# Second gating layer of the second cycle in three fp32r passes, with the first half's first turn moved between first-layer tiles

## What is computed

```python
def _coupling_net(h, w1, b1, w2, b2, w3, b3, w4, b4):      # 512 -> 512 -> 256 -> 128 -> 1
    h = _gelu(h @ w1 + b1)
    h = _gelu(h @ w2 + b2)
    h = _gelu(h @ w3 + b3)
    return jax.nn.sigmoid(h @ w4 + b4)

gf = _global_net(x.mean(axis=1, keepdims=True), ...)
out = x
for _ in range(3):
    tf = _coupling_net(out, ...)
    combined = 0.7 * gf + 0.3 * tf
    coupling = 0.1 + adaptive_range * (combined - 0.5) * 2.0
    out = out + coupling * _twist(out)
```

## Time and profile before

| | before |
|---|---|
| runs, median (lowest to highest) | 1707.92 us (1707.28 to 1707.93) |
| profiled execution: its time, its span | 1706.81 us, 1705.0 us |
| granted TensorE clock, mean | 0.998 |
| TensorE matmuls busy | 1680.3 us (99%) |
| VectorE busy | 1475.7 us (87%) |
| ScalarE busy | 1272.9 us (75%) |
| GpSimd busy | 680.1 us (40%) |

### The profile page before, as it was taken

The page is one execution under the profiler, slowest core; times in us unless marked ns, Lnnn a source line. Parts: engine busy times, 40 slices in busy tenths (PEclk is TensorE's granted clock), DMA queues, the critical chain, the costliest instruction groups (busy, mean ns, idle before and its releaser), DMA issues. The chain is left out here.

```text
span 1705.0 us, 33568 instructions
## 1 busy us (share of the span) xinstructions
PE 1680.3 (99%) x12344; PEld 1283.1 (75%) x12344; DVE 1475.7 (87%) x2615; ACT 1272.9 (75%) x2249; POOL 680.1 (40%) x649
## 2 busy tenths in 40 slices
PE   8999999999999999999999999999999999999997
PEld 7888887777777777777777777777786685775864
DVE  6666666999999999999999999999788978969968
ACT  4233235999999999999999999999765576466556
POOL 3545443332388552586432785465323010100100
PEclk9999999999999999999999999999999999999999
DMA  9989966765477754667764675666515313412301
GB/s 317 355 309 333 340 248 177 170 168 135 140 190 183 142 140 107 149 204 143 162 150 121 150 198 128 142 134 154 182 35 160 91 50 99 139 50 52 113 26 50
DMA packets 165922, 270.09 MB, mean 158 GB/s; under 512 B 26736, under 2 KB 79216, under 8 KB 165760
## 3 DMA queue, kind: packets, MB, share of 16 engines
q1 hardware_dynamic: 110416, 158.84, 29.3%
q0 software_dynamic: 54768, 108.05, 27.0%
q10 hardware_dynamic: 576, 1.05, 0.2%
HBM read 179.48 MB, written 84.21 MB: 155 GB/s over the span
## 5 line engine op out<-in xcount | busy, mean ns | idle before, releaser
L1103 DVE CUSTOM_DVE_ANT_0 a_neg<-a_sc_ps,am 128x1024 f32<-128x1024 f32 x512 | 621.9, 1215 | 2.0 <-PE a_sc_ps L935 1.8
L1043 ACT ACTIVATE a_prob<-a_neg,a_row_min 128x1024 f32<-128x1024 f32 x512 | 585.6, 1144 | 14.7 <-DVE a_row_min L1103 8.6
L949 PEld LDWEIGHTS a_tr_ps<-ident,a_prob 128*128 128x128 f32 x4096 | 461.1, 140 | 89.2 <-issue 53.2
L949 PE MATMUL a_tr_ps<-ident,a_prob 128*128 128x128 f32 x4096 | 519.8, 274 | 0.9 <-ACT a_probT L1021 0.9
L1078 DVE COPY a_probT<-a_tr_ps 128x512 f32<-128x512 f32 x512 | 350.6, 685 | 36.9 <-PE a_tr_ps L949 35.3
L1021 ACT ACTIVATE a_probT<-a_tr_ps 128x512 f32<-128x512 f32 x512 | 303.8, 594 | 35.7 <-PE a_tr_ps L949 16.0
L831 POOL DMA_DIRECT2D a_q_st<-q_parts x144 | 79.5, 557 | 166.5 <-PE a_sc_ps L935 131.6
L935 PE MATMUL a_sc_ps<-k_first,a_q_st 96*128 96x512 f32 x384 | 126.3, 427 | 0.1
L935 PE MATMUL a_sc_ps<-a_k_st,a_q_st 96*128 96x512 f32 x384 | 126.0, 426 | 0.0
L969 PE MATMUL a_o_ps<-a_probT,a_v 128*32 128x256 f32 x2048 | 123.6, 382 | 0.6 <-ACT a_o L1032 0.6
L969 PE MATMUL a_o_ps<-a_probT,v_first 128*32 128x256 f32 x2048 | 123.8, 382 | 0.0
(11 more groups left out here) (246 smaller groups left out, 3299.7 us busy)
## 6 DMA issues: line engine op xcount, KB each, us to landing
a_q_st<-q_parts POOLq DMA_DIRECT2D x144, 128.0 KB, 3.9
k_first<-k_parts POOLq DMA_DIRECT2D x24, 512.0 KB, 8.4
a_k_st<-k_parts POOLq DMA_DIRECT2D x24, 512.0 KB, 7.6
a_m_raw<-mask SPq DMA_DIRECT2D x24, 512.0 KB, 4.9
a_adj_raw<-adj SPq DMA_DIRECT2D x24, 512.0 KB, 6.0
k_parts<-p_out_hi SPq DMA_DIRECT2D x32, 256.0 KB, 4.0
k_parts<-p_out_lo SPq DMA_DIRECT2D x32, 256.0 KB, 5.2
v_all<-p_v_out SPq DMA_DIRECT2D x8, 1024.0 KB, 4.8
```

The costliest lines, as they stand in the source:

```text
L949: last = pe.transpose(tr_ps[:, bank(u, half), j * P:(j + 1) * P], prob[:, r % NPROB, t * P:(t + 1) * P], ident[:])
L1043: act.activation(prob[:, r % NPROB, :], neg[:, r % 2, :], ACT.Exp, scale=-1.0, bias=row_min[:, r % 2:r % 2 + 1], accum_out=row_sum[:, r // ...
L1103: dve.tensor_tensor_reduce(out=neg[:, r % 2, :], in0=sc_ps[:, r % 2, :], in1=am[:, 2 * qb + qt, :], scale=-1.0, scalar=3.4e38, op0=ALU.add ...
```

## The change

The second cycle's second layer is done in three passes too. ScalarE makes two Gelus of each of its tiles (high part to `u_hi_second`, whole value to `u_second`, which lies in the memory of `u_hi`), and VectorE subtracts them in `split_u(b, 1, j)`. The first turn (n = 0, j = 0) moves ahead: its `layer2` stands after the second half's first-layer tile 1 and accumulates in `tr`, its `layer3` stands after tile 2 and writes to `z4`, its `layer4` after tile 3. ScalarE's and VectorE's lists follow. For k = 1 to 4 ScalarE's list now has all tiles of `h1` of the next turn ahead of `h2_half` of turn k. VectorE's list is regular: `second_cycle`, two tiles of `turned`, `split_u`, two tiles of `turned`. Two loads wait for a later turn. Cut to its core:

```diff
-    SPLIT = (0, 2)
+    SPLIT = (0, 1, 2)
-        h1_second = [... f_h1_second{j} ... F32, offset=SB_AM + 8192 * j ...]
+        u_hi_second = [... f_u_hi_second{j} ... F32R, offset=SB_AM + 8192 * j ...]
+        u_second = [... f_u_second{j} ... F32, offset=u_hi_at[j] ...]
+        u_lo_second = [... f_u_lo_second{j} ... F32R, offset=u_hi_at[j] ...]
...
-                            sp.wait_ge(z2_ready, 2 * turn(b, 0, 0) + 2)
+                            sp.wait_ge(z2_ready, 2 * turn(b, 1, 0) + 2)
...
-                    pool.wait_ge(z2_ready, 2 * turn(b - 1, 0, 1) + 2)
+                    pool.wait_ge(z2_ready, 2 * turn(b - 1, 1, 1) + 2)
...
             def layer2(b, n, j, tiles):
+                out = tr if n == 0 and j == 0 else acc[:, 2 * j:2 * j + 2]
                 if n == 0 and 0 in tiles:
                     if j == 0:
-                        pe.wait_ge(own_read, 2 * ET * NJ * (b + 1))
+                        pe.wait_ge(xT_lo_ready, ET * NJ * (b + 1))
                     else:
                         pe.wait_ge(shared_read, 4 * ET * NJ * (b + 1))
...
-                            last = pe.matmul(acc[:, 2 * j + m, :], w2[:, t, ms], h1_second[j][:, t, :], start=t == 0, stop=t == ET - 1)
+                        last = three_pass(pe, out[:, m, :], w_hi[:, t, ms], w_lo[:, t, ms], high[:, t, :], low_part[:, t, :],
+                                          t == 0, t == ET - 1)
...
                 global_layer1(b, 1)
+                layer2(b, 0, 0, (0, 1))
+                global_layer2(b)
+                layer2(b, 0, 0, (2, 3))
+                global_layer3(b)
                 first_layer(b, 1, 2)
+                layer3(b, 0, 0)
                 first_layer(b, 1, 3)
-                layer2(b, 0, 0, (0,))
-                global_layer2(b)
-                for k in range(NJ * CYCLES):
+                layer4(b, 0, 0)
+                layer2(b, 0, 1, (0,))
+                for k in range(1, NJ * CYCLES):
                     n, j = k // NJ, k % NJ
                     layer2(b, n, j, (1, 2, 3))
-                    if k == 0:
-                        global_layer3(b)
                     layer3(b, n, j)
...
-                if n == 1:
-                    act.activation(h1_second[j][:, m, :], u[j][:, m, :], ACT.Gelu, ...).then_inc(h1_ready, 1)
-                    return
-                act.activation(u_hi_third[j][:, m, :], ...)
-                act.activation(u[j][:, m, :], ...).then_inc(h1_ready, 1)
+                act.activation((u_hi_second if n == 1 else u_hi_third)[j][:, m, :], ...)
+                act.activation((u_second if n == 1 else u)[j][:, m, :], ...).then_inc(h1_ready, 1)
...
                 first_cycle_h1(b, 1, 1)
                 act.wait_ge(gz2_ready, b + 1)
                 act.activation(g2[:], z4[:, 1, 2:3], ACT.Gelu, bias=small.gb2[:]).then_inc(g2_ready, 1)
+                act.wait_ge(gz3_ready, b + 1)
+                act.activation(g_tanh[:], z4[:, 1, 3:4], ACT.Tanh, ...).then_inc(g3_ready, 1)
+                h2_half(b, 0, 0, 0)
+                h2_half(b, 0, 0, 1)
+                read_own(b, 1, 2)
+                h3_all(b, 0, 0)
+                first_cycle_h1(b, 1, 2)
+                read_own(b, 1, 3)
                 first_cycle_h1(b, 1, 3)
-                for k in range(NJ * CYCLES):
+                gate(b, 0, 0)
+                for k in range(1, NJ * CYCLES):
                     n, j = k // NJ, k % NJ
-                    if k == 3:
-                        next_h1(0)
+                    if k <= NJ * (CYCLES - 1):
+                        for m in range(ET):
+                            h1(b, (k - 1) // NJ + 1, (k - 1) % NJ, m)
                     h2_half(b, n, j, 0)
                     h2_half(b, n, j, 1)
-                    next_h1(1 if k == 3 else 0)
                     h3_all(b, n, j)
-                    if k < 3:
-                        next_h1(1, 2)
-                        gate(b, n, j)
-                        next_h1(3)
-                        continue
-                    if k == 4:
-                        next_h1(1)
-                    next_h1(2, 3)
...
                 split_w2(b)
+                split_u(b, 0, 0)
                 add_shared(b, 1, 1)
-                add_shared(b, 1, 2)
-                split_u(b, 0, 0)
-                add_shared(b, 1, 3)
-                split_u(b, 0, 1)
+                split_u(b, 0, 1, (0, 1))
                 dve.wait_ge(g3_ready, b + 1)
                 dve.tensor_scalar(base[:], ...).then_inc(base_ready, 1)
+                add_shared(b, 1, 2)
+                split_u(b, 0, 1, (2,))
+                add_shared(b, 1, 3)
+                split_u(b, 0, 1, (3,))
...
                         second_cycle(b, j)
-                        turned(b, 0, ((0, 1, 2), (3,))[j])
-                        if j:
-                            turned(b, 1, (0, 1))
+                        turned(b, j, (0, 1))
+                        split_u(b, 1, j)
+                        turned(b, j, (2, 3))
                     elif n == 1:
                         third_cycle(b, j)
-                        if j == 0:
-                            turned(b, 1, (2,))
-                        split_u(b, 2, j, (1,))
-                        if j == 0:
-                            turned(b, 1, (3,))
-                        split_u(b, 2, j, (2, 3))
+                        split_u(b, 2, j, (1, 2, 3))
```

More of the change, by code:

```diff
@@ L1159, in ffn_phase @@
         pair_lo = sb("f_pair_lo", [P, 2, CH], F32R)
-        h1_second = [nc.alloc_sbuf_tensor_at(f"f_h1_second{j}", [P, ET, CH], F32, offset=SB_AM + 8192 * j) for j in range(NJ)]
+        u_hi_second = [nc.alloc_sbuf_tensor_at(f"f_u_hi_second{j}", [P, ET, CH], F32R, offset=SB_AM + 8192 * j) for j in range(NJ)]
+        u_second = [nc.alloc_sbuf_tensor_at(f"f_u_second{j}", [P, ET, CH], F32, offset=u_hi_at[j]) for j in range(NJ)]
+        u_lo_second = [nc.alloc_sbuf_tensor_at(f"f_u_lo_second{j}", [P, ET, CH], F32R, offset=u_hi_at[j]) for j in range(NJ)]
         u_hi_third = [nc.alloc_sbuf_tensor_at(f"f_u_hi_third{j}", [P, ET, CH], F32R, offset=SB_AM + 8192 * j) for j in range(NJ)]
@@ L1494, in layer3 @@
                     pe.wait_ge(h2_ready, 2 * k + t + 1)
-                    last = pe.matmul(tr[:, j, :], w3[:, t, :], h2[j][:, t, :], start=t == 0, stop=t == 1)
+                    last = pe.matmul((z4 if n == 0 and j == 0 else tr)[:, j, :], w3[:, t, :], h2[j][:, t, :], start=t == 0, stop=t == 1)
                 last.then_inc(z3_ready, 1)
@@ L1500, in layer4 @@
                 pe.wait_ge(h3_ready, k + 1)
-                if n == 0:
+                if n == 0 and j == 1:
                     pe.wait_ge(g3_ready, b + 1)
@@ L1621, in h1 @@
                 act.wait_ge(u_ready, ET * k + m + 1)
-                if n == 1:
-                    act.activation(h1_second[j][:, m, :], u[j][:, m, :], ACT.Gelu, bias=small.b1[:, m:m + 1]).then_inc(h1_ready, 1)
-                    return
-                act.activation(u_hi_third[j][:, m, :], u[j][:, m, :], ACT.Gelu, bias=small.b1[:, m:m + 1])
-                act.activation(u[j][:, m, :], u[j][:, m, :], ACT.Gelu, bias=small.b1[:, m:m + 1]).then_inc(h1_ready, 1)
+                act.activation((u_hi_second if n == 1 else u_hi_third)[j][:, m, :], u[j][:, m, :], ACT.Gelu, bias=small.b1[:, m:m + 1])
+                act.activation((u_second if n == 1 else u)[j][:, m, :], u[j][:, m, :], ACT.Gelu, bias=small.b1[:, m:m + 1]).then_inc(h1_ready, 1)
             def h2_half(b, n, j, m):
                 act.wait_ge(z2_ready, 2 * turn(b, n, j) + m + 1)
-                act.activation(h2[j][:, m, :], acc[:, 2 * j + m, :], ACT.Gelu, bias=small.b2[:, m:m + 1]).then_inc(h2_ready, 1)
+                source = tr[:, m, :] if n == 0 and j == 0 else acc[:, 2 * j + m, :]
+                act.activation(h2[j][:, m, :], source, ACT.Gelu, bias=small.b2[:, m:m + 1]).then_inc(h2_ready, 1)
             def h3_all(b, n, j):
                 act.wait_ge(z3_ready, turn(b, n, j) + 1)
-                act.activation(h2[j][:, 0, :], tr[:, j, :], ACT.Gelu, bias=small.b3[:]).then_inc(h3_ready, 1)
+                act.activation(h2[j][:, 0, :], (z4 if n == 0 and j == 0 else tr)[:, j, :], ACT.Gelu, bias=small.b3[:]).then_inc(h3_ready, 1)
             def gate(b, n, j):
@@ L1682, in batch @@
                 first_cycle_h1(b, 1, 0)
-                read_own(b, 1, 2)
-                first_cycle_h1(b, 1, 1)
-                read_own(b, 1, 3)
                 act.wait_ge(gz1_ready, b + 1)
@@ L1689, in batch @@
                 last.then_inc(g1_ready, 1)
-                first_cycle_h1(b, 1, 2)
+                first_cycle_h1(b, 1, 1)
                 act.wait_ge(gz2_ready, b + 1)
                 act.activation(g2[:], z4[:, 1, 2:3], ACT.Gelu, bias=small.gb2[:]).then_inc(g2_ready, 1)
+                act.wait_ge(gz3_ready, b + 1)
+                act.activation(g_tanh[:], z4[:, 1, 3:4], ACT.Tanh, scale=0.5, bias=small.half_gb3[:]).then_inc(g3_ready, 1)
+                h2_half(b, 0, 0, 0)
```

(16 more changed lines are left out.)

20 lines of the change are left out of this document (6 added, 14 removed).

## The result

The changed kernel takes 1813.78 us (median of 4 runs, 1813.46 to 1814.58); the kernel before, on the same chip, 1707.6 us. The ratio is 1.062, with a 95% interval from 1.0605 to 1.0642: slower by 106 us. The forecast was 1788, its range 1767 to 1820. The mechanism came as forecast; how often the clock fell, and what each fall cost, did not.

What follows compares the result with a forecast made beforehand. TensorE was taken as the bound, only just, in the gating turns; the change makes them serial. 1706.8 us profiled plus 68 (serial rounds) plus 12 (clock) gave 1786.8, with 1.1 for the median 1788; range 1767 to 1820.

Steps and rivals of the forecast that it cites:

- Part 1: TensorE's second-cycle second-layer tiles: three passes save 11.3 us of its work, but this buys nothing in the serial rounds.
- Part 2: More work in the second cycle: two Gelus a tile on ScalarE, eight subtractions on VectorE, 4.8 us a batch.
- Part 3: Moved first turn: beta 0.6 us later, about 1.1 us new idle for shared_read, no cost from moved queues.
- T: The end of the last first-layer tile on TensorE, expected to move from 1406.72 to about 1414.7 us.
- Part 4: ScalarE's four h1 tiles ahead of h2 make turns serial: rounds 13.4, 13.1, 13.1, 9.4 us; 68 us lost.
- that case: Rival: TensorE's clock holds through the short gaps, giving 1776 us; chance 0.33.
- The clock: TensorE's clock falls to half in every second of 16 new gaps, 1.5 us each: 12 us.
- nearly every gap: Rival: TensorE's clock falls in nearly all new gaps, 1.5 to 4.1 us each, giving 1800 to 1842; chance 0.12.
- The upper bound: Largest clock cost: all serial matmuls behind each of 16 gaps at half speed, 4.1 us each, 66 us.
- The rival without the order: h1 tiles don't hold layer3; only VectorE's added 4.8 us a batch show, list 39.8 us: 1714; chance 0.05.
- Faster: Rival: sums come early enough that the Gelus finish when layer2 ends, TensorE stays the bound: 1702 us; chance 0.04.

Runs made afterwards that it cites:

- E8: Kernel before with three passes alone; ScalarE does all four h1 tiles ahead of the gate, VectorE sets turned between subtractions and defers part: 1730.54 us, ratio 1.014.
- E3: Changed kernel with 19 useless matmuls filling TensorE's gap ahead of layer3 at k = 1 to 4: 1781.1 us.
- E10: Changed kernel with GpSimd's last split_weighted moved ahead of keep_w2, away from batch 0's second cycle: 1814.43 us.
- E1: Changed kernel with ScalarE doing both halves of h2 ahead of the next turn's h1 Gelus again: 1792.88 us, ratio 1.0502.
- E5: Kernel before with the second cycle in three passes, first turn and ScalarE's order unmoved, VectorE subtracting right behind second_cycle: 1782.03 us, ratio 1.0438.
- E3b: Changed kernel with 9 useless matmuls in each gap ahead of layer3 at k = 1 to 4: 1794.2 us.
- E2: Kernel before, second cycle still plain fp32, with only ScalarE's four h1 tiles moved ahead of h2 at k = 1 to 4: 1796.41 us.

## Why the prediction was right, and where it was not

- **Part 1, cheaper tiles.** That they buy nothing was right: `layer2` ends and TensorE stands idle for 4.7 to 5.2 us. E8 shows the same for the kindest order.
- **Part 2.** The 4.8 us a batch on VectorE were right (4.98 in E8). In the changed kernel they lie beside waits and cost nothing there.
- **Part 3, the prologue.** Beta is ready at 1448.8, T + 4.9 (T + 4.75 predicted); the idle time for `shared_read` is 1.10 us, four times, as worked out. Costs were put at none for the moved queues, and none of their loads stands among TensorE's waits.
- **Part 4, the order.** The step that decided was right: gaps of 4.7 to 5.2 us (one of 7.2 in batch 0), all put down to h2 behind four tiles of `h1`. E3 gives the rounds without the clock, 13.5, 13.2, 13.2 and 9.5 us. Its 1781.1 stands against 1776 for that case. Of these 5 us some 1.6 are the one fall that E3 keeps (15.17 against 13.52), so 3.5 are the rounds' own. Most of them, some 2.5 us, lie in batch 0, where GpSimd slowed VectorE (E10). That contention was not in the sum, and the rows of batch 1 couldn't show it. The rest is 0.45 a batch in the rounds and 0.3 from T to the first `layer3` (12.58 against 12.3), of which the time up to T gives some back.
- **The clock**, the mis-sized term. I took a fall in every second gap at 1.5 us, 12 us. It fell in all 16, at 2.1 us, 34 us. Both halves of the choice were too low. Each gap was known to be longer than the 3.3 us (3.4 by the same rows) after which it had fallen once, and the rounds are alike, so "nearly every gap" deserved more than 0.12; this case gave 1800 to 1842, and 1814 lies in it. The upper bound, 4.1 us a fall, wasn't reached: a part of each low stretch lay in the idle time, and the clock came back within `layer2`. The 22 us missing here and the 3.5 of part 4 are the distance from 1788 to 1814. The rule of the Trainium skill that the prediction cites (TensorE: Matmul & The Clock Gate, Part 1, "HAM oscillation") held in kind: bursts between waits went to half speed in each round, 16 of 16.
- **The rival without the order, 1714.** The chance of 0.05 stands, its price doesn't. VectorE's list was put at 39.8 us. In the kernel before it already spans 37.6 us (1418.83 to 1456.46), its waits for the last Gelus among it, so with 4.8 it is 42.4, and E8 measured 42.6. That gives some 1724 to 1727, and only with VectorE's list rebuilt. With the order merely put right (E1) or never touched (E5) it is 1782 to 1793. That is what I hadn't seen: splitting the second cycle gives VectorE a step behind ScalarE's Gelus, and any Gelu behind the gate then closes a second loop.
- **Faster, 1702**: no run came near it; the kernel before stays the fastest. Its condition, beta 6.9 us ahead of the end of `layer2`, wasn't tried.

## What to carry to other kernels

Before trading TensorE's passes for splits, write down each engine's list in order and look for an operation that waits for an engine which waits, further down its own list, for this one: each extra hand-over (ScalarE to VectorE here) can close such a loop, and its length, not the busy time, is the price. When serial rounds leave TensorE idle for 4.7 us or more each, cost the clock as falling in every one, as it did here; with gaps of 2.7 to 3.2 us it fell in some and not in others. The mean price here was 2.1 us, about half of the 4.1 us of serial matmuls behind the gap. If the gaps can't be removed, useless matmuls in them are a cheap remedy and a measurement of the clock's share (33 us here, with one fall left).

## What the runs showed of the hardware

- The clock came back late by differing amounts: in the changed kernel it was low for 6.8 us at ten gaps and for 3.4 us at six, in E10's last batch once for 13.7 us, until 12 us behind the end of the gap. Gaps of 2.7 to 3.2 us were followed by half speed in some batches and not in others (E3, E3b, E2).
- VectorE's 128x512 operations took 2.1 to 2.5 times as long (2.74 against 1.30 us for two, 1.75 against 0.69) beside three GpSimd tensor operations, which in turn took 1.6 us instead of 1.3. With that work moved, both went back (E10). The Trainium skill (SBUF — State Buffer, "Who interferes with whom") has it that a VectorE instruction with two inputs in SBUF contends with a GpSimd one that reads SBUF, and these are such instructions; the trace agrees. In E10 the same GpSimd operations lay beside four of VectorE's additions with one input in PSUM (`add_shared`), and neither was slowed: 0.68 and 1.3 us.
